# Message passing layer on one core: transposes at the end of TensorE's last nine steps, own banks for the last node layers and sums

## The chip, the cores and the metric

The kernel runs on one core of a Trainium2 chip. The time is what the device takes for one execution, in microseconds, and the result for a kernel is the median of its runs. All numbers are float32.

## The reference

A graph has 12,500 nodes with 64 features and 200,000 edges, sorted by destination. Cut to what matters:

```python
def ssp(x): return softplus(x) - log(2)
nodes = x[edges].reshape(200000, 128)            # source row, destination row
gates = ssp(edge_attr @ We1 + be1) @ We2 + be2
gates = gates * (1 - sigmoid(5 * (edge_weight1 - 3.5)))
h = ssp(nodes @ Wn1 + bn1) @ Wn2 + bn2
message_sum = zeros((12500, 64)).at[dst].add(h * gates)
new = x + (ssp(message_sum @ Ws1 + bs1) @ Ws2 + bs2)
out = layernorm(x + new, axis=-1, eps=1e-5)
```

## The kernel before

**Steps.** The edges are worked off in 391 quads of 512 (NQ = 391; the last has 320 edges). The five engines run their own programs, written out by hand in the order in which each executes, and meet at semaphores. In step s the engines work on neighbouring quads:

- GpSimd gathers the source rows of a quad from DRAM with four indirect DMAs (L449) into a ring of 16 places (`ga`), up to 15 quads ahead of the transposes.
- SyncE loads edge features (`ea`), the destinations relative to a window (`relb`) and the windows' shares of the first node layer (`bw`), two quads at a time.
- TensorE: `transposes(q)` (L561 for edge features, L563 for gathered rows) into bank 4 of PSUM, `front(q)` (L609, the first node layer of the edge, and the gates' first layer in `gates_in`, L571), `mid(q)` (second layers, L622 and L626) into bank 6 or 5, and `back(q)` (L639), which sums the messages of a quad over a window of 64 nodes by a one-hot matrix, into bank 7.
- ScalarE: `evacuate(q)` copies the transposed quad to SBUF (L818), `sizes(q)` (L826, L828) and `logs(q)` (L835 to L841) work out the softplus of the first layers, `fill(q)` (L847) writes the biases of the second layers into their bank.
- VectorE: `pick` (L1062) and `one_hot` (L1068) make the one-hot matrices, `hidden(q)` (L1076, L1080) the first layers' output, `message(q)` (L1087, L1095) the product with the gates, and `flush(q)` (L1114) adds the window's sums to `acc`, at a place that is read from a table (L1102).

TensorE's step s is front(s), transposes(s + 2), back(s - 3), mid(s - 1). ScalarE's step s is sizes(s), evacuate(s + 2), logs(s), fill(s).

**Node layer.** The nodes are in 25 groups of 500 (NG = 25). Since edges are sorted, a group is complete long before the last edge, and from step 206 (NODE0) each eight steps (STEPS) carry the node layer of one group: in the step at offset 0 TensorE's `node_hidden` (L648), between the front's L609 and its gates L571, with ScalarE's `node_sizes` (L886, L887) and `node_log` (L891, L893) in the same step; at offset 2 VectorE's `node_hidden` (L1194); at offset 3 TensorE's `node_out` (L657), at 4 VectorE's `node_add` (L1200), at 5 ScalarE's square (L897), at 6 VectorE's sum (L1204) and ScalarE's root (L902, L904), at 7 VectorE's scaling (L1212 to L1220). SyncE then stores the group.

**The tail.** Steps up to 381 run in loops; steps 382 (TAIL0) to 393 are written out. Step 382 is offset 0 of group 22, step 390 offset 0 of group 23, whose other pieces, and group 24 (the last), follow after the last step. Group 24's node layer needs the sums of all quads. The sums are in `ps_s` (bank 7), node_hidden writes into banks 0 and 1 behind the columns of the even quads' first layers (`ps_h`), node_out into banks 2 and 3 behind those of the odd quads (`ps_y`). The end of TensorE's program:

```python
                for s in range(TAIL0, NQ + 3):
                    fast_step(s, s % ARING, group_at(s))
                node_out(NG - 2)
                pe.wait_ge(flushed, NQ)
                node_hidden(NG - 1)
                node_out(NG - 1)
```

A branch for inputs that are not sorted closely enough (`general_step`) isn't taken here.

## Time and profile before

| | before |
|---|---|
| median of 3 runs | 2000.88 us (2000.53 to 2002.76) |
| the profiled execution | 2002.99 us, its span 2001.1 us |
| TensorE busy, mean granted clock | 1730.7 us (86%), 0.953 |
| ScalarE busy | 1532.0 us (77%) |
| GpSimd busy | 1485.6 us (74%) |
| VectorE busy | 1285.7 us (64%) |
| last gather begins | 1966.65 us |

The profile lists for each engine when its instructions began, in us from the start of the span, and what ended the idle time before them. In such a row a group of like instructions stands as one ("x8"). A duration in a row can overlap the start of the next operation on the same engine by up to 0.13 us; where the text speaks of the time that an operation takes of its engine's queue, it is the distance to the next start. "issue" as a releaser means that the profile shows nothing that was waited for. The granted clock of TensorE is 1.0 at 2.4 GHz and 0.5 at 1.2 GHz.

### The profile page before, as it was taken

To read this page: it belongs to the slowest core of one execution; us is meant where nothing else is said; L and a number is where in the kernel's file an instruction comes from. 1 tells how busy PE (TensorE), PEld (TensorE's weight loads), DVE (VectorE), ACT (ScalarE), POOL (GpSimd) and SP (SyncE) were. 2 spreads that over 40 slices of the span, in tenths; PEclk is the share of its full clock that TensorE was granted. 3 is DMA by queue.
4 is the path that set the end of the run, shared out by engine and by line. 5 is a ranking of instruction groups with operands and counts; after the bars stand their busy time and mean duration, and the time that the engine had idled before them with its cause. 6 is when DMAs were issued, how large, how long until landed. Compare 5 with 4: busy or idle time off the path is not lost.

```text
span 2001.1 us, 53540 instructions
## 1 busy us (share of the span) xinstructions
PE 1730.7 (86%) x16249; PEld 1323.6 (66%) x16249; DVE 1285.7 (64%) x3512; ACT 1532.0 (77%) x3368; POOL 1485.6 (74%) x1572
## 2 busy tenths in 40 slices
PE   4699999888888888888889889888888988898887
PEld 3477777766666666666666666666666666666665
DVE  4578887666665655566656666666666666666665
ACT  2589998877777777777777877787878777787785
POOL 6777777777777777777777777777777777777772
PEclk7799999999899999999999999999999999999998
DMA  5433343333333333333333333333333333333331
GB/s 120 121 86 97 96 96 97 84 85 83 80 76 70 74 73 72 73 72 73 72 73 74 77 76 71 78 76 70 81 75 74 73 76 73 71 82 75 73 74 31
DMA packets 255904, 157.77 MB, mean 79 GB/s; under 512 B 44873, under 2 KB 226518, under 8 KB 255838
## 3 DMA queue, kind: packets, MB, share of 16 engines
q1 hardware_dynamic: 202124, 104.94, 18.0%
q0 software_dynamic: 50048, 51.35, 15.9%
q10 hardware_dynamic: 3666, 0.68, 0.2%
q8 instruction: 32, 0.52, 0.1%
q14 instruction: 34, 0.28, 0.0%
HBM read 146.94 MB, written 9.87 MB: 78 GB/s over the span
## 4 chain that ended last, share of the span: by engine, by line
POOL 59%; issue 22%; PE 11%; DVE 3%; SPq 2%; ACT 1%; DMA 1%; ACTq 1%; DVEq 1%; POOLq 0%
POOL ga L449 59%; PE ps L609 3%; PE ps L622 3%; PE ps L626 1%; SPq L331 1%; PE ps L571 1%; PE ps L561 1%; PE ps L639 1%; DVE hid L1076 1%; DMA ga<-in_x_dram,srcT 1%; DVE hid L1080 1%; PE ps L563 1%; DMA w_tab<-w_i 0%; SPq L326 0%; SPq L317 0%
## 5 line engine op out<-in xcount | busy, mean ns | idle before, releaser
L449 POOL DMA_INDIRECT ga<-in_x_dram,srcT x1564 | 1484.6, 949 | 481.3 <-issue 473.0
L826 ACT ACTIVATE lg<-ps,bn1c 128x512 f32<-128x512 f32 x391 | 268.5, 687 | 305.3 <-PE ps L571 272.8
L622 PE MATMUL ps<-wn,hid 128*128 128x64 f32 x3128 | 445.1, 287 | 19.2 <-DVE hid L1080 16.5
L1076 DVE SCALAR_TENSOR_TENSOR hid<-ps,neg_b,lg 128x512 f32<-128x512 f32 x391 | 292.9, 749 | 228.5 <-ACT lg L841 214.4
L622 PEld LDWEIGHTS ps<-wn,hid 128*128 128x128 f32 x3128 | 390.2, 196 | 51.2 <-DVE hid L1080 24.9
L561 PE MATMUL ps<-ident,ea 128*128 128x128 f32 x782 | 172.4, 303 | 216.8 <-DMA ga<-in_x_dram,srcT 147.8
L818 ACT COPY xe<-ps 128x512 f32<-128x512 f32 x391 | 229.9, 588 | 124.0 <-PE ps L563 109.0
L609 PE MATMUL ps<-xe,wn 64*128 64x256 f32 x1564 | 289.5, 449 | 0.0
L561 PEld LDWEIGHTS ps<-ident,ea 128*128 128x128 f32 x782 | 79.8, 143 | 301.5 <-issue 283.9
L626 PE MATMUL ps<-we,hid 128*128 128x128 f32 x1564 | 272.2, 299 | 0.0
L1114 DVE TENSOR_TENSOR acc<-acc,ps 64x64 f32 x782 | 168.2, 215 | 161.8 <-issue 155.3
L1068 DVE TENSOR_TENSOR oh<-ps,relT 128x256 f32<-128x256 f32 x391 | 163.9, 419 | 164.7 <-PE ps L639 144.0
L835 ACT ACTIVATE lg<-lg 128x512 f32<-128x512 f32 x391 | 251.8, 644 | 0.0
L609 PE MATMUL ps<-ohT,bw 64*128 64x256 f32 x1564 | 246.9, 394 | 0.0
L839 ACT ACTIVATE lg<-lg 128x512 f32<-128x512 f32 x391 | 245.7, 628 | 0.0
L847 ACT COPY ps<-bsum 128x512 f32<-128x512 f32 x391 | 232.6, 595 | 0.0
L626 PEld LDWEIGHTS ps<-we,hid 128*128 128x128 f32 x1564 | 216.9, 201 | 0.0
L1080 DVE SCALAR_TENSOR_TENSOR hid<-ps,neg_b,lg 128x256 f32<-128x256 f32 x391 | 185.7, 475 | 0.0
L1062 DVE TENSOR_SCALAR ohT<-relb,iota_p 128x256 f32<-128x256 uint8 x391 | 148.6, 380 | 55.5 <-PE ps L571 48.9
L828 ACT ACTIVATE lg<-ps,be1c 128x256 f32<-128x256 f32 x391 | 182.8, 467 | 0.0
L639 PE MATMUL ps<-oh,msg 128*64 128x64 f32 x3128 | 179.6, 237 | 1.3 <-DVE acc L1114 1.3
L571 PE MATMUL ps<-xe,we 64*64 64x128 f32 x3128 | 180.6, 302 | 0.0
(124 smaller groups left out, 1848.5 us busy)
## 6 DMA issues: line engine op xcount, KB each, us to landing
ea<-in_edge_attr_dram SPq DMA_DIRECT2D x195, 256.0 KB
ga<-in_x_dram,srcT POOLq DMA_INDIRECT x1564
bw<-b_tab SPq DMA_DIRECT2D x782, 32.0 KB
relb<-rel_tab SPq DMA_DIRECT2D x196, 64.0 KB
b_tab<-share SPq DMA_DIRECT2D x25, 250.0 KB
out_dram<-xs SPq DMA_DIRECT2D x25, 125.0 KB
xs<-in_x_dram SPq DMA_DIRECT2D x3, 750.0 KB
rows_i<-in_dst_dram SPq DMA_DIRECT2D x1, 768.0 KB
```

The source lines that it names most:

```text
L449: pool.indirect_dma_start(to[:, t % 2, t // 2, :], None, x, bass.IndirectOffsetOnAxis(ap=idx[:, t:t + 1], axis=0)).then_inc(done, 16)
L561: pe.transpose(ps_xe[:, k * P:(k + 1) * P], ea[:, u, k, :], ident[:, :])
L609: pe.matmul(ps[:, 2 * (u % 2) + k, 0:PAIR], weights, rows, start=(end == 0), stop=(end == 1), skip_group_check=True)
L622: pe.matmul(hg[:, t * D:(t + 1) * D], hid[:, u % 2, t * P:(t + 1) * P], wn2[:, :], start=False, stop=False, skip_group_check=True)
L626: mm = pe.matmul(gates[:, :, j, :], hid[:, u % 2, QUAD + j * P:QUAD + (j + 1) * P], we2[:, :].rearrange("p (k d) -> p k d", k=2), start=Fa ...
L818: act.copy(xe[:, u, :, :].rearrange("p h e -> p (h e)"), ps_xe[:, :]).then_inc(xe_e, 1)
L826: act.activation(lg[:, u % 2, 0:QUAD].rearrange("p (k e) -> p k e", k=2), z[:, :, 0:PAIR], ACT.Abs, bias=bn1c[:, 0:1]).then_inc(n_abs, 1)
L835: act.activation(ln_n, ln_n, ACT.Exp, scale=-1.0).then_inc(n_exp, 1)
L839: act.activation(ln_n, ln_n, ACT.Ln, bias=1.0)
L847: act.copy(hg, bsum[:, :, :, :].rearrange("p h k d -> p (h k d)")).then_inc(filled, 1)
L1076: dve.scalar_tensor_tensor(out=hid[:, u % 2, 0:QUAD].rearrange("p (k e) -> p k e", k=2), in0=ps[:, 2 * (u % 2):2 * (u % 2) + 2, 0:PAIR], s ...
L1080: dve.scalar_tensor_tensor(out=hid[:, u % 2, QUAD:QUAD + PAIR].rearrange("p (j e) -> p j e", j=2), in0=ps[:, 2 * (u % 2):2 * (u % 2) + 2, ...
```

## The change

In TensorE's steps 382 to 390 the transposes move to the end of the step and are those of the next quad instead of the one after it; step 382 has none, since step 381 already made those of 383. ScalarE's copy moves in the same way behind fill and node step. Step 390 carries no node step any more. The node layer of group 23 comes after back(388) on TensorE and writes into banks 2 and 3 (`ps_h_end`), its outputs into 0 and 1 (`ps_y_end`); the sums of quad 390 go to bank 4 (`ps_s_end`), which the transposes no longer need. VectorE loads the places of the last three quads together and takes the last operations in a new order.

```diff
+        ps_h_end = ps[:, 2:4, 3 * P:3 * P + PB]
+        ps_y_end = ps[0:PB, 0:2, 3 * P:4 * P]
+        ps_s_end = ps[:, 4, :]
...
-            def back(q, u):
+            def back(q, u, sums=ps_s):
...
-                if reached(q, 1):
+                if reached(q, 1) and sums is ps_s:
                     pe.wait_ge(flushed, q)
...
-                for s in range(TAIL0, NQ + 3):
-                    fast_step(s, s % ARING, group_at(s))
-                node_out(NG - 2)
+                for s in range(TAIL0, NQ):
+                    front(s, s % ARING, group_at(s) if s < NQ - 1 else None)
+                    back(s - 3, (s - 3) % RING)
+                    mid(s - 1, (s - 1) % RING, ps_hg[(s - 1) % 2])
+                    if TAIL0 < s < NQ - 1:
+                        transposes(s + 1, (s + 1) % ARING)
+                back(NQ - 3, (NQ - 3) % RING)
+                pe.wait_ge(flushed, NQ - 1 - BACK)
+                node_hidden(NG - 2, ps_h_end)
+                back(NQ - 2, (NQ - 2) % RING)
+                mid(NQ - 1, (NQ - 1) % RING, ps_hg[(NQ - 1) % 2])
+                node_out(NG - 2, ps_y_end)
+                back(NQ - 1, (NQ - 1) % RING, ps_s_end)
                 pe.wait_ge(flushed, NQ)
-                node_hidden(NG - 1)
-                node_out(NG - 1)
+                pe.wait_ge(h_relu, NG - 1)
+                node_hidden(NG - 1, ps_h_end)
+                node_out(NG - 1, ps_y_end)
...
                 for q in range(TAIL0, NQ):
-                    fast_step(q, q % RING, group_at(q))
+                    node = group_at(q) if q < NQ - 1 else None
+                    sizes(q, q % RING)
+                    if node is not None and node[1] == 0:
+                        node_sizes(node[0])
+                    logs(q, q % RING)
+                    fill(q, ps_hg[q % 2], 2)
+                    if node is not None:
+                        node_step(*node)
+                    if TAIL0 < q < NQ - 1:
+                        evacuate(q + 1, (q + 1) % RING)
+                node_sizes(NG - 2, ps_h_end)
+                node_log(NG - 2)
                 node_square(NG - 2)
-                node_sizes(NG - 1)
+                node_sizes(NG - 1, ps_h_end)
...
-                for s in range(TAIL0, NQ + 3):
+                for s in range(TAIL0, NQ):
                     fast_step(s, s % RING, group_at(s))
-                node_add(NG - 2)
+                load_places(NQ - 3, 3)
+                message(NQ - 2, (NQ - 2) % RING, ps_hg[(NQ - 2) % 2])
+                one_hot(NQ - 1, (NQ - 1) % RING)
+                flush(NQ - 3, 0)
+                hidden(NQ - 1, (NQ - 1) % RING)
+                flush(NQ - 2, 1)
+                node_hidden(NG - 2)
+                message(NQ - 1, (NQ - 1) % RING, ps_hg[(NQ - 1) % 2])
+                flush(NQ - 1, 2, ps_s_end)
+                node_add(NG - 2, ps_y_end)
                 node_sum(NG - 2)
                 node_hidden(NG - 1)
                 node_scale(NG - 2)
-                node_add(NG - 1)
+                node_add(NG - 1, ps_y_end)
```

TensorE in step 388 before: front (L609, L571), transposes of quad 390 (L561, L563), back(385) (L639), mid(387) (L622, L626). `ps` is PSUM; the other names are the operands.

```order
L609 MATMUL ps<-xe,wn 128x256 x2
L609 MATMUL ps<-ohT,bw 128x256 x2
L571 MATMUL ps<-xe,we 64x128 x4
L561 MATMUL ps<-ident,ea 128x128 x2
L563 MATMUL ps<-ident,ga 128x128 x2
L639 MATMUL ps<-oh,msg 64x64 x4
L622 MATMUL ps<-wn,hid 128x64 x4
L626 MATMUL ps<-we,hid 128x2x64 x2
```

The same step after: front (L613, L575), back(385) (L643), mid(387) (L626, L630), then the transposes of quad 389 (L565, L567), and the next front.

```order
L613 MATMUL ps<-xe,wn 128x256 x2
L613 MATMUL ps<-ohT,bw 128x256 x2
L575 MATMUL ps<-xe,we 64x128 x4
L643 MATMUL ps<-oh,msg 64x64 x4
L626 MATMUL ps<-wn,hid 128x64 x4
L630 MATMUL ps<-we,hid 128x2x64 x2
L565 MATMUL ps<-ident,ea 128x128 x2
L567 MATMUL ps<-ident,ga 128x128 x2
L613 MATMUL ps<-xe,wn 128x256 x2
L613 MATMUL ps<-ohT,bw 128x256 x2
```

The transposes have moved from before back and mid to behind them, and are of one quad less ahead.

ScalarE in step 388 before: sizes (L826, L828), the copy of quad 390 (L818), logs (L835 to L841), fill (L847), the root of group 22 (L902, L904).

```order
L826 ACTIVATE lg<-ps,bn1c 128x512
L828 ACTIVATE lg<-ps,be1c 128x256
L818 COPY xe<-ps 128x512
L835 ACTIVATE lg<-lg 128x512
L837 ACTIVATE lg<-lg 128x256
L839 ACTIVATE lg<-lg 128x512
L841 ACTIVATE lg<-lg 128x256
L847 COPY ps<-bsum 128x512
L902 ACTIVATE lvar<-svar,epsb 125x4
L904 ACTIVATE rstd<-lvar 125x4
```

The same step after: sizes (L842, L844), logs (L851 to L857), fill (L863), root (L918, L920), then the copy of quad 389 (L834), and the next step's first operation.

```order
L842 ACTIVATE lg<-ps,bn1c 128x512
L844 ACTIVATE lg<-ps,be1c 128x256
L851 ACTIVATE lg<-lg 128x512
L853 ACTIVATE lg<-lg 128x256
L855 ACTIVATE lg<-lg 128x512
L857 ACTIVATE lg<-lg 128x256
L863 COPY ps<-bsum 128x512
L918 ACTIVATE lvar<-svar,epsb 125x4
L920 ACTIVATE rstd<-lvar 125x4
L834 COPY xe<-ps 128x512
L842 ACTIVATE lg<-ps,bn1c 128x512
```

The copy has moved from between sizes and logs to behind everything of the step, and is of the quad whose front comes next.

TensorE's last part before, from the node layer inside front 390 on (L648 is node_hidden, L657 node_out; "L639 x8" are back(389) and back(390)):

```order
L648 MATMUL ps<-acc,ws1d 128x125 x4
L571 MATMUL ps<-xe,we 64x128 x4
L639 MATMUL ps<-oh,msg 64x64 x4
L622 MATMUL ps<-wn,hid 128x64 x4
L626 MATMUL ps<-we,hid 128x2x64 x2
L639 MATMUL ps<-oh,msg 64x64 x4
L622 MATMUL ps<-wn,hid 128x64 x4
L626 MATMUL ps<-we,hid 128x2x64 x2
L639 MATMUL ps<-oh,msg 64x64 x8
L657 MATMUL ps<-ws2d,hidn 125x128 x2
L648 MATMUL ps<-acc,ws1d 128x125 x4
L657 MATMUL ps<-ws2d,hidn 125x128 x2
```

After, from the end of front 390, back(387), on (L652 is node_hidden, L661 node_out):

```order
L643 MATMUL ps<-oh,msg 64x64 x4
L626 MATMUL ps<-wn,hid 128x64 x4
L630 MATMUL ps<-we,hid 128x2x64 x2
L643 MATMUL ps<-oh,msg 64x64 x4
L652 MATMUL ps<-acc,ws1d 128x125 x4
L643 MATMUL ps<-oh,msg 64x64 x4
L626 MATMUL ps<-wn,hid 128x64 x4
L630 MATMUL ps<-we,hid 128x2x64 x2
L661 MATMUL ps<-ws2d,hidn 125x128 x2
L643 MATMUL ps<-oh,msg 64x64 x4
L652 MATMUL ps<-acc,ws1d 128x125 x4
L661 MATMUL ps<-ws2d,hidn 125x128 x2
```

node_hidden of group 23 has gone from inside the front of step 390 to behind back(388), mid(390) has come behind back(389), and back(390) behind node_out.

## Rows read from the trace of the kernel before

**Rows 1.** The page: chain that ended last by engine; costliest group of instructions.

```profile
POOL 59%; issue 22%; PE 11%; DVE 3%; SPq 2%; ACT 1%; DMA 1%; ACTq 1%; DVEq 1%; POOLq 0%
...
L449 POOL DMA_INDIRECT ga<-in_x_dram,srcT x1564 | 1484.6, 949 | 481.3 <-issue 473.0
```

**Rows 2.** Timeline (start us, us, instruction, idle before), GpSimd's last gather; transposes on TensorE.

```profile
1966.65 0.94 POOL L449 DMA_INDIRECT ga<-in_x_dram,srcT  x1 [0.30 <-issue]
...
1960.69 0.41 PE L561 MATMUL ps<-ident,ea 128*128 128x128 f32 x2 [1.02 <-issue]
...
1969.16 0.41 PE L561 MATMUL ps<-ident,ea 128*128 128x128 f32 x2 [0.53 <-issue]
```

**Rows 3.** Timeline, TensorE: transposes(383); front 389, back, mid, front 390.

```profile
1935.19 0.44 PE L561 MATMUL ps<-ident,ea 128*128 128x128 f32 x2
...
1971.63 0.70 PE L609 MATMUL ps<-xe,wn 64*128 64x256 f32 x4
...
1973.08 0.45 PE L639 MATMUL ps<-oh,msg 128*64 128x64 f32 x8
1973.46 1.11 PE L622 MATMUL ps<-wn,hid 128*128 128x64 f32 x8
...
1974.99 0.70 PE L609 MATMUL ps<-xe,wn 64*128 64x256 f32 x4
```

**Rows 4.** Windows: stretch, engines' busy us (x instructions), PEclk, DMA share, GB/s.

```profile
1980.00:1990.00 10.00, 6.28 (x46) 5.52 (x45) 4.89 (x16) 3.18 (x8) 0.00 (x0) 0.64 0.00 0
```

**Rows 5.** Timeline, TensorE's last part.

```profile
1983.18 1.97 PE L622 MATMUL ps<-wn,hid 128*128 128x64 f32 x8 [2.41 <-DVE hid L1080]
...
1986.04 0.70 PE L639 MATMUL ps<-oh,msg 128*64 128x64 f32 x8
...
1989.68 1.97 PE L648 MATMUL ps<-acc,ws1d 128*128 128x125 f32 x8
1993.83 1.22 PE L657 MATMUL ps<-ws2d,hidn 128*125 128x128 f32 x4 [2.19 <-DVE hidn L1194]
```

**Rows 6.** Timeline, VectorE: hidden(390), message(390), last operation.

```profile
1982.65 0.48 DVE L1080 SCALAR_TENSOR_TENSOR hid<-ps,neg_b,lg 128x256 f32<-128x256 f32 x1
...
1986.61 0.42 DVE L1095 TENSOR_TENSOR msg<-ps,gcut 128x256 f32<-128x256 f32 x1
...
1997.60 0.42 DVE L1220 TENSOR_TENSOR xs<-xs,rsq 125x256 f32<-125x256 f32 x1
```

**Rows 7.** Timeline, ScalarE in steps 387 to 389.

```profile
1968.33 0.42 ACT L897 ACTIVATE sq<-xs 125x256 f32<-125x256 f32 x1
...
1969.82 0.58 ACT L818 COPY xe<-ps 128x512 f32<-128x512 f32 x1
...
1971.97 0.59 ACT L847 COPY ps<-bsum 128x512 f32<-128x512 f32 x1
1972.48 0.29 ACT L902 ACTIVATE lvar<-svar,epsb 125x4 f32<-125x4 f32 x1
1972.81 0.20 ACT L904 ACTIVATE rstd<-lvar 125x4 f32<-125x4 f32 x1
1973.21 0.69 ACT L826 ACTIVATE lg<-ps,bn1c 128x512 f32<-128x512 f32 x1 [0.20 <-PE ps L571]
...
1975.81 0.59 ACT L847 COPY ps<-bsum 128x512 f32<-128x512 f32 x1
```

**Rows 8.** Timeline, ScalarE: first operation of step 383.

```profile
1946.31 0.67 ACT L826 ACTIVATE lg<-ps,bn1c 128x512 f32<-128x512 f32 x1
```

**Rows 9.** Timeline, TensorE: node output of group 22 in step 385.

```profile
1953.31 0.70 PE L657 MATMUL ps<-ws2d,hidn 128*125 128x128 f32 x4
```

**Rows 10.** Timeline, TensorE: first and last of 80 gaps of 1.2 us; a window.

```profile
336.54 0.44 PE L561 MATMUL ps<-ident,ea 128*128 128x128 f32 x2 [1.29 <-DMA ga<-in_x_dram,srcT]
...
1929.69 0.43 PE L561 MATMUL ps<-ident,ea 128*128 128x128 f32 x2 [1.24 <-DMA ga<-in_x_dram,srcT]
...
1932.00:1934.00 2.00, 2.00 (x10) 1.60 (x11) 1.35 (x3) 1.53 (x5) 1.58 (x2) 0.50 0.21 33
```

More of the change, by code:

```diff
@@ L638, in back, with node_hidden @@
                     for k in range(2):
-                        mm = pe.matmul(ps_s[k * D:(k + 1) * D, 0:W], msg[:, u % 2, 2 * k + j, :],
+                        mm = pe.matmul(sums[k * D:(k + 1) * D, 0:W], msg[:, u % 2, 2 * k + j, :],
                                        oh[:, u, 2 * k + j, :], start=(j == 0), stop=(j == 1))
                 mm.then_inc(sc_mm, 1)
-            def node_hidden(g):
+            def node_hidden(g, hidden_units=ps_h):
                 sums = acc[:, bass.ds(g * GN, GN)].rearrange("f (p b) -> f b p", b=4)
@@ L647, in node_hidden, with node_out @@
                     for c in range(2):
-                        mm = pe.matmul(ps_h[:, c, :], ws1d[:, h, :, :].rearrange("f i d -> f (i d)"), sums[:, 2 * h + c, :],
+                        mm = pe.matmul(hidden_units[:, c, :], ws1d[:, h, :, :].rearrange("f i d -> f (i d)"), sums[:, 2 * h + c, :],
                                        start=(h == 0), stop=(h == 1), skip_group_check=True)
                 mm.then_inc(h_mm, 1)
-            def node_out(g):
+            def node_out(g, y=ps_y):
                 pe.wait_ge(h_b, g + 1)
@@ L656, in node_out @@
                 for c in range(2):
-                    mm = pe.matmul(ps_y[:, c, :], hidn[:, c * PB:(c + 1) * PB],
+                    mm = pe.matmul(y[:, c, :], hidn[:, c * PB:(c + 1) * PB],
                                    ws2d[:, :, :].rearrange("f h d -> f (h d)"), start=True, stop=True)
@@ L1104, in load_places, with flush @@
                     skip_runtime_bounds_check_because=IN_RANGE)
-            def flush(q, at):
+            def flush(q, at, sums=ps_s):
                 firsts = places[2 * at:2 * at + 2]
@@ L1114, in flush @@
                     ins = dve.tensor_tensor(acc[half, bass.ds(firsts[k], W)], acc[half, bass.ds(firsts[k], W)],
-                                            ps_s[half, 0:W], ALU.add)
+                                            sums[half, 0:W], ALU.add)
                 ins.then_inc(flushed, 1)
@@ L1199, in node_add @@
                 rows = xs[0:PB, bass.ds(g * 4, 4), :].rearrange("p (h c) d -> p c h d", c=2)
-                dve.tensor_tensor(rows, ps_y.rearrange("p c (h d) -> p c h d", h=2), rows, ALU.add).then_inc(y_add, 1)
+                dve.tensor_tensor(rows, y.rearrange("p c (h d) -> p c h d", h=2), rows, ALU.add).then_inc(y_add, 1)
             def node_sum(g):
```

8 lines of the change are left out of this document (4 added, 4 removed).

## The prediction

> **What bounds the kernel now.** I read the page first, then the windows, then the timelines of the last 70 us engine by engine. The page's chain gives GpSimd 59%: the pace is one gather after another, 0.95 us busy and 0.30 us of issue, four to a step, 5.0 us a step [rows 1, 2]. The last gather starts at 1966.65 and its quad (390) is transposed at 1969.16, 2.51 us later; for quad 388, whose last gather started two steps of 5.0 earlier, that distance was 4.03 us (to 1960.69) [rows 2]. What follows the last gather, 34.5 us to the end of the span, has no gather to wait for. There the reader is to see three pieces: fronts 389 and 390, which follow each other on TensorE without a gap (1971.63, 1974.99) [rows 3]; the end of the pipe, where TensorE idles 2.41 us before mid(390), the mean granted clock is 0.64, and matmuls run at 1.2 GHz (L622 takes 1.97 us instead of 1.11) [rows 3 to 5]; and the node layer of the last group, from L648 at 1989.68 to VectorE's last operation at 1997.60 + 0.42 = 1998.02 [rows 5, 6]. 3.08 us of store follow to 2001.1.
>
> **The change, part 1: transposes last, evacuation last.** Before, TensorE transposes quad s + 2 inside step s, and ScalarE copies it (L818) between sizes and logs of step s: ready a whole step before its front, so no front waits for it. After, the transposes of s + 1 stand at the end of step s, and ScalarE copies them after logs and fill of s. So front(s + 1) waits for a copy that stands behind all of ScalarE's work of step s, and that work waits for front(s). This closes a loop, priced by rows. From the start of a front to ScalarE's first operation on it: 1971.63 to 1973.21, 1.58 us [rows 3, 7]. Sizes and logs, 1973.21 to 1975.81, 2.60; the fill L847, 1971.97 to 1972.48, 0.51; the copy L818 0.58, and 0.04 until TensorE sees it (as from the end of L1080 at 1983.13 to L622 at 1983.18), 0.62 [rows 5 to 7]. The loop is 1.58 + 2.60 + 0.51 + 0.62 = **5.31 us** a step. TensorE's own work in a step is front 1.45, back 0.38, mid 1.53, transposes about 0.6: they end 3.96 us after the front's start, ahead of the copy's turn at 4.69 [rows 2, 3]. So ScalarE's order decides, and TensorE idles about 1.35 us in each step.
>
> Where it starts: TensorE's step 382 has the same front and node layer in both kernels. ScalarE no longer has a copy in step 382 (0.58, of which 0.11 overlap the next operation), so sizes(383) begin at 1946.31 - 0.47 = 1945.84 [rows 7, 8]. Sizes, logs, fill, + 3.11, and the copy, + 0.62: front(384) at 1949.57. Then six loops of 5.31 to front(390), and on the same path the node output of group 22 in step 385 (L657, 0.70 less 0.07 of overlap), the square L897 (0.42 less 0.06) and the root, L902 and L904 (1972.48 to 1972.81 + 0.20, and a hand-over of 0.04) [rows 7, 9]: 1949.57 + 31.86 + 0.63 + 0.36 + 0.57 = **1982.99**, against 1974.99: 8.0 us later. By then quad 390 has been in SBUF for over 10 us: that a late gather no longer holds back TensorE's other work is worth nothing here, since a loop of 5.31 is no faster than the gathers' 5.0.
>
> **Part 2: the node layer of group 23 out of step 390.** Before, L648 stood between front and gates of 390, 1.97 us as at 1989.68 [rows 5]; after, it comes behind back(388). ScalarE's start on quad 390 goes from 1974.99 + 1.97 + 1.58 = 1978.54 to 1982.99 + 1.58 = 1984.57: of the 8.0 us, 6.0 are left.
>
> **Part 3: the order of the last sums.** By TensorE's new order, from front(390)'s end at 1984.43: back(387) 0.38, mid(389) 1.53, back(388) 0.38, L648 1.97, back(389) 0.38, to 1989.07. mid(390) needs hid(390): ScalarE's logs end at 1984.57 + 2.60 + 0.14 of tail = 1987.31, but VectorE first does message(389), one-hot(390) and flush(388) behind mid(389)'s end at 1986.34, some 1.7 us, and then 1.15 for L1076 and L1080: 1989.25. TensorE waits 0.2 instead of 2.41 us, stays at 2.4 GHz, and mid(390) takes 1.53 instead of the 2.86 from L622 at 1983.18 to L639 at 1986.04 [rows 5]: to 1990.78. The node output waits for VectorE's hidn until about 1990.8 and ends at 1991.45. message(390), two operations of 0.42 and their hand-over, ends near 1991.76 [rows 6], back(390) at 1992.25, flush(390) 0.5 later, and L648 of the last group starts at **1992.8** against 1989.68. So this part gives back 2.9 of the 6.0 us: 1.3 by the clock in mid(390), the rest because sums and node layer lie in what was idle. The bank of its own for the last sums takes away back(390)'s wait for flush(389), which ends before message(390) does: nothing. What hides it is message(390); without that cover it were 0.5.
>
> From L648 to VectorE's end, 8.34 us before [rows 5, 6], nothing is reordered; the doubt is L657, 1.22 at 1.2 GHz, 0.70 at 2.4 [rows 5, 9]. The end is + 2.6 to + 3.1; I take + 2.9.
>
> **Part 4: the clock.** Before, TensorE's gaps stood in the loop of the gathers, which hid a slow spell. In the trace TensorE idled at least 1.2 us in one piece 80 times between 336 and 1930 us, first and last in [rows 10]; after 23 of them the granted clock fell from 1.0 to 0.5 within 4 us, as after the last (0.50 in the window from 1932), and stayed there 4 to 6 us. The new loop has seven gaps of 1.1 to 1.9 us: by that share two falls, and fewer because a slow step fills its own gap. A fall now lies on the path. At 1.2 GHz mid takes 2.86, back 0.70 and transposes and gates about twice their time, 1.0 and 0.6 [rows 5]; with the fall one us into a front, the transposes end at 1.06 + 0.6 + 0.70 + 2.86 + 1.0 = 6.2 us after its start instead of the copy's turn at 4.69: + 1.5, and up to 2.4 if the next front is slow too. I take one fall, + 1.5.
>
> The Trainium skill ("TensorE: Matmul & The Clock Gate", section "HAM oscillation — how this bites in real kernels") has it that only idle stretches longer than any in this loop bring the clock down. By that rule no fall would come and the time would be 2003.3, rival 1 below; the last gap of [rows 10], 1.24 us and the clock down behind it, speaks against it.
>
> **Part 5: the start.** In this execution TensorE came out of a slow spell into step 382. transposes(383) ran at 1935.19; its last gather began seven steps of 5.0 before 1966.65, at 1931.65, and by the distances 2.51 and 4.03 it could have run at 1934.2 to 1935.7 [rows 2, 3]. The new loop passes such a shift on, the old one absorbed it: between - 1.0 and + 0.5, I take - 0.5.
>
> **Sum.** 2.9 + 1.5 - 0.5 = + 3.9 us. The profiled execution took 2002.99 us for a span of 2001.1, and the median of the runs is 2.1 lower, 2000.88; the difference of the tails is added to the median: **2004.8**.
>
> **Rivals.**
> 1. No fall of the clock in the new loop: 2000.88 + 2.4 = 2003.3. For it: 57 of the 80 gaps passed without.
> 2. Two or more falls: 2004.8 + 1.5 = 2006.3, three 2007.8. For it: a gap in every step, longest where square and root are added. It decides from the second fall on.
> 3. The faster side: the loop is hidden, because ScalarE is through with a step before the transposes of the next are. If the fronts stay where they are, front(390) at 1974.99, parts 2 and 3 are pure gain, 8.0 - 2.9 = 5.1 us: 1995.8. If they come as soon as the transposes allow (1969.16 + 0.6 + 0.62 = 1970.4), it is 4.6 us less, 1991.2. The draw lies at front(390) = 1980.1, a loop of (1980.1 - 1949.57 - 1.56) / 6 = 4.83 us; faster by over 4 us needs 4.2. For it: fronts 389 and 390 were 3.36 us apart in the old order [rows 3]. Against: no copy stood between them, and ScalarE's rows alone hold 3.7 of the loop, the front 1.58 [rows 7].
> 4. The loop is some tenths shorter than my sum, near those 4.83: 2000.9, no change. It needs an overlap that no row shows.
>
> **How the numbers follow.** Forecast, one fall: 0.33; rival 1: 0.25; rival 2: 0.31; rival 3: 0.05; rival 4: 0.06. A measurement of this kernel tells 0.2%, 4.0 us, from no change. The forecast lies at that bound; I put 0.18 of its 0.33 within and 0.15 beyond. Within: 0.18 + 0.25 + 0.06 = 0.49; slower: 0.15 + 0.31 = 0.46; faster 0.05. Range: down to rival 1 with the start's - 1.0 and the end's + 2.6, which is 2002.5, and one us less for the spread of a median, 2001.5; up to three falls of which one is of the dearer kind, 2009.
>
> **What would show it.** In the changed kernel the copies L834 begin behind the fill L863 in steps 383 to 389, TensorE idles 1.1 to 1.9 us before each front, the fronts are 5.3 us apart and front(390) starts about 16 us behind the last gather; TensorE waits under 0.7 us for hid(390). Fronts under 4.6 us apart, or idle time there that ends at a gather, would prove the forecast wrong; a clock of 1.0 throughout with 5.3 a step is rival 1.

## The result

The changed kernel takes **2011.2 us** (median of 8 runs, 2005.8 to 2016.5), the kernel before 2000.7 us (8 runs, 2000.0 to 2002.8). The ratio of their runs is 1.0046 with a 95% interval of 1.0037 to 1.0055: slower, and clear of noise (the two medians by themselves give 1.0052). The forecast was 2004.8 us with a range up to 2009. The direction of its sum was right, the size was not: + 3.9 us forecast, + 10.5 measured by the medians.

The profiled execution of the changed kernel took 2007.65 us (span 2004.8), one of the shorter ones. Its rows show the loop of the forecast almost to the hundredth. TensorE's fronts in the timeline (start us, us, instruction, the idle time before it and what ended it):

```profile
1946.88 0.70 PE L613 MATMUL ps<-xe,wn 64*128 64x256 f32 x4 [1.63 <-ACT xe L834]
...
1952.21 0.70 PE L613 MATMUL ps<-xe,wn 64*128 64x256 f32 x4 [1.47 <-ACT xe L834]
...
1958.18 0.70 PE L613 MATMUL ps<-xe,wn 64*128 64x256 f32 x4 [1.47 <-ACT xe L834]
...
1963.51 0.70 PE L613 MATMUL ps<-xe,wn 64*128 64x256 f32 x4 [1.47 <-ACT xe L834]
...
1969.14 0.76 PE L613 MATMUL ps<-xe,wn 64*128 64x256 f32 x4 [1.76 <-ACT xe L834]
```

From 1958.18 to 1963.51 is 5.33 us, and each front now waits for ScalarE's copy. On ScalarE the same step:

```profile
1959.76 0.69 ACT L842 ACTIVATE lg<-ps,bn1c 128x512 f32<-128x512 f32 x1 [1.63 <-PE ps L575]
...
1962.35 0.59 ACT L863 COPY ps<-bsum 128x512 f32<-128x512 f32 x1
1962.87 0.59 ACT L834 COPY xe<-ps 128x512 f32<-128x512 f32 x1
```

The copy follows the fill and ScalarE then waits 1.6 us for the next front: neither engine is full, each waits for the other. Before, the same fronts had no gap in front of them [rows 3]. Behind the fifth of these gaps the clock fell; the windows (columns as in [rows 4]) and the rows of two slow steps:

```profile
1960.00:1970.00 10.00, 6.77 (x66) 5.63 (x64) 6.18 (x17) 7.46 (x17) 4.78 (x5) 0.98 0.14 30
1970.00:1980.00 10.00, 9.32 (x62) 6.56 (x61) 4.40 (x15) 5.01 (x12) 0.00 (x0) 0.51 0.04 13
```

```profile
1971.94 1.97 PE L626 MATMUL ps<-wn,hid 128*128 128x64 f32 x8
...
1976.40 1.23 PE L613 MATMUL ps<-xe,wn 64*128 64x256 f32 x4 [0.68 <-ACT xe L834]
...
1982.93 0.70 PE L613 MATMUL ps<-xe,wn 64*128 64x256 f32 x4 [1.13 <-ACT xe L834]
```

These two steps took 7.26 us (from 1969.14) and 6.53 us, where 5.75 and 5.33 are due: 2.7 us lost by one fall (5.75 and 5.33 us are the lengths of the same two steps in e7, e14 and e17 below, where the clock stayed at 2.4 GHz). The end of the kernel, which answers to [rows 5]:

```profile
1989.48 1.10 PE L626 MATMUL ps<-wn,hid 128*128 128x64 f32 x8 [0.39 <-DVE hid L1107]
...
1992.15 0.45 PE L643 MATMUL ps<-oh,msg 128*64 128x64 f32 x8 [0.56 <-DVE msg L1122]
1993.24 2.04 PE L652 MATMUL ps<-acc,ws1d 128*128 128x125 f32 x8 [0.64 <-DVE acc L1141]
1997.47 1.22 PE L661 MATMUL ps<-ws2d,hidn 128*125 128x128 f32 x4 [2.19 <-DVE hidn L1221]
```

mid(390) waits 0.39 us instead of 2.41 and runs in 1.10 instead of 1.97; L652 starts 10.3 us after front 390 (1982.93), against 14.7 before. The last gather, on GpSimd:

```profile
1965.05 0.94 POOL L453 DMA_INDIRECT ga<-in_x_dram,srcT  x1 [0.30 <-issue]
```

The span of 2004.8 us ended 39.75 us behind it, against 34.45 before: 5.3 us longer.

### The profile page after: what moved, and what is told of

Read it like the earlier page. It is cut to its first block, busy times and chain, and to the rows that moved or that the text cites. A ratio compares the mean times of both kernels' runs of the same rounds, so it can differ in the third digit from the quotient of the medians.

```text
span 2004.8 us, 53539 instructions
## 1 busy us (share of the span) xinstructions
PE 1744.5 (87%) x16249; PEld 1333.0 (66%) x16249; DVE 1286.6 (64%) x3512; ACT 1532.5 (76%) x3368; POOL 1484.1 (74%) x1572
## 3 DMA queue, kind: packets, MB, share of 16 engines
q0 software_dynamic: 50048, 51.35, 14.8%
## 4 chain that ended last, share of the span: by engine, by line
POOL 57%; issue 21%; PE 11%; DVE 3%; ACT 3%; DMA 2%; SPq 1%; ACTq 1%; DVEq 1%; POOLq 0%
POOL ga L453 57%; PE ps L613 3%; PE ps L626 2%; DMA ga<-in_x_dram,srcT 1%; PE ps L630 1%; PE ps L575 1%; SPq L335 1%; DVE hid L1103 1%; PE ps L565 1%; DVE hid L1107 1%; PE ps L643 1%; PE ps L567 1%; ACT xe L834 0%; ACT lg L851 0%; PE ps L652 0%
## 5 line engine op out<-in xcount | busy, mean ns | idle before, releaser
L842 ACT ACTIVATE lg<-ps,bn1c 128x512 f32<-128x512 f32 x391 | 268.7, 687 | 321.1 <-PE ps L575 286.7
L626 PE MATMUL ps<-wn,hid 128*128 128x64 f32 x3128 | 449.1, 288 | 21.0 <-DVE hid L1107 19.3
L626 PEld LDWEIGHTS ps<-wn,hid 128*128 128x128 f32 x3128 | 394.1, 198 | 53.8 <-DVE hid L1107 30.2
L565 PE MATMUL ps<-ident,ea 128*128 128x128 f32 x782 | 173.2, 304 | 196.8 <-DMA ga<-in_x_dram,srcT 143.0
L834 ACT COPY xe<-ps 128x512 f32<-128x512 f32 x391 | 230.1, 589 | 114.8 <-PE ps L567 101.3
L613 PE MATMUL ps<-xe,wn 64*128 64x256 f32 x1564 | 292.3, 452 | 9.6 <-ACT xe L834 9.6
L630 PE MATMUL ps<-we,hid 128*128 128x128 f32 x1564 | 274.4, 300 | 0.0
L565 PEld LDWEIGHTS ps<-ident,ea 128*128 128x128 f32 x782 | 80.5, 143 | 280.0 <-issue 263.6
L851 ACT ACTIVATE lg<-lg 128x512 f32<-128x512 f32 x391 | 251.9, 644 | 0.0
L613 PE MATMUL ps<-ohT,bw 64*128 64x256 f32 x1564 | 249.0, 397 | 0.0
L863 ACT COPY ps<-bsum 128x512 f32<-128x512 f32 x391 | 232.9, 596 | 0.0
L630 PEld LDWEIGHTS ps<-we,hid 128*128 128x128 f32 x1564 | 219.0, 202 | 0.0
L844 ACT ACTIVATE lg<-ps,be1c 128x256 f32<-128x256 f32 x391 | 182.9, 468 | 0.0
L643 PE MATMUL ps<-oh,msg 128*64 128x64 f32 x3128 | 180.8, 238 | 0.6 <-DVE msg L1122 0.6
L575 PE MATMUL ps<-xe,we 64*64 64x128 f32 x3128 | 181.1, 303 | 0.0
```

What stands on the lines that cost most here:

```text
L565: pe.transpose(ps_xe[:, k * P:(k + 1) * P], ea[:, u, k, :], ident[:, :])
L613: pe.matmul(ps[:, 2 * (u % 2) + k, 0:PAIR], weights, rows, start=(end == 0), stop=(end == 1), skip_group_check=True)
L626: pe.matmul(hg[:, t * D:(t + 1) * D], hid[:, u % 2, t * P:(t + 1) * P], wn2[:, :], start=False, stop=False, skip_group_check=True)
L630: mm = pe.matmul(gates[:, :, j, :], hid[:, u % 2, QUAD + j * P:QUAD + (j + 1) * P], we2[:, :].rearrange("p (k d) -> p k d", k=2), start=Fa ...
L834: act.copy(xe[:, u, :, :].rearrange("p h e -> p (h e)"), ps_xe[:, :]).then_inc(xe_e, 1)
L842: act.activation(lg[:, u % 2, 0:QUAD].rearrange("p (k e) -> p k e", k=2), z[:, :, 0:PAIR], ACT.Abs, bias=bn1c[:, 0:1]).then_inc(n_abs, 1)
```

## The experiments

The chips differ. On the first and on chip 14 the kernel before takes 2001 to 2003 us, on chips 6, 11 and 15 it takes 2512 to 2544 us, with no gather in the way at the end. So each kernel is compared with runs of the kernel before on its own chip. What can be compared across chips are the steps of the tail: at the same clock, and with no gather in the way, they have the same length to 0.02 us everywhere. The table gives, from the profile of each, the time from front 382 to front 390, from there to the last group's node layer on TensorE (L648 before, L652 after), from there to the end of the span, and their sum; then the time of the runs against the kernel before on that chip.

| run | kernel | 382 to 390 | to L652 | to end | sum | ratio (95%) |
|---|---|---|---|---|---|---|
| before | before, first chip | 37.3 | 14.7 | 11.4 | 63.4 | |
| e5 | before, chip 15 | 34.6 | 13.8 | 11.0 | 59.4 | 0.9989 (0.9973 to 1.0004) |
| after | changed, 1 fall | 47.9 | 10.3 | 11.6 | 69.8 | 1.0046 (1.0037 to 1.0055) |
| e1 | changed, 2 falls, chip 11 | 49.2 | 10.3 | 11.5 | 71.0 | 1.0043 (1.0028 to 1.0059) |
| e6 | changed, 1 short fall, chip 15 | 46.4 | 10.3 | 11.6 | 68.3 | 1.0049 (1.0027 to 1.0071) |
| e13 | changed, 1 short fall, chip 11 | 46.3 | 10.3 | 11.5 | 68.2 | 1.0057 (1.0036 to 1.0078) |
| e16 | changed, slow for 5 of 8 steps, chip 6 | 53.6 | 14.8 | 11.6 | 79.9 | 1.0034 (1.0020 to 1.0049) |
| e2 | + 4 fillers, chip 11 | 46.0 | 10.3 | 11.5 | 67.8 | 1.0035 (1.0020 to 1.0050) |
| e7 | + 3 fillers, chip 15 | 45.2 | 10.3 | 11.5 | 67.1 | 1.0022 (1.0005 to 1.0039) |
| e14 | + 3 fillers, chip 11 | 45.2 | 10.3 | 11.5 | 67.0 | 1.0023 (1.0013 to 1.0034) |
| e17 | + 3 fillers, chip 6 | 45.2 | 10.3 | 11.5 | 67.0 | 1.0021 (1.0007 to 1.0036) |
| e11 | new steps, old end, chip 14 | 53.5 | 14.5 | 11.5 | 79.5 | 1.0052 (1.0038 to 1.0066) |
| e3 | old steps, new end, chip 11 | 34.6 | 10.8 | 11.5 | 56.9 | 0.9990 (0.9977 to 1.0004) |
| e12 | the same, 1 fall, chip 14 | 39.0 | 10.8 | 11.5 | 61.3 | 0.9984 (0.9975 to 0.9993) |
| e4 | one ahead, early copy, chip 11 | 34.4 | 10.8 | 11.5 | 56.7 | 0.9986 (0.9968 to 1.0003) |
| e8 | the same, chip 15 | 34.4 | 10.8 | 11.5 | 56.8 | 0.9986 (0.9971 to 1.0002) |
| e15 | the same, chip 11 | 34.4 | 10.8 | 11.5 | 56.7 | 0.9997 (0.9987 to 1.0007) |
| e18 | late transposes, early copy, chip 6 | 44.5 | 11.5 | 11.5 | 67.5 | 1.0024 (1.0008 to 1.0040) |

**The changed kernel again (e1, e6, e13, e16).** No edit.

> The changed kernel once more, for another profile of it: eight executions took 2005.8 to 2016.5 us, and the profiled one (2007.65) had one stretch of TensorE at 1.2 GHz in the tail, 1969.7 to 1979.7 us. Theory A (the clock is on the path since the gaps stand in the loop): the excess over 2000.7 us follows the time that TensorE spends at 1.2 GHz after 1940 us; at 2.4 GHz the loop is 5.33 us a step in every execution; an execution near 2011 shows some 20 us of half clock there, one near 2016 nearly all of the tail. Theory B (something else differs between executions, the landing of gathers or the state in which step 382 begins): the slow executions show longer waits on DMA or a later front 382, with the clock as in the profile that we have. Median expected 2008 to 2012 by both.

> The changed kernel on the same chip. In its two profiles the tail from front 382 to the end of the span was 69.8 and 71.0 us, with one stretch at 1.2 GHz each (and a short second one in the later), and each such stretch cost 2.2 us (two steps of 6.94 and 6.53 us instead of 5.90 and 5.33). Theory A (clock falls add up): ratio 1.004 to 1.005, and this profile's tail is 67.6 us + 2.2 us for each fall that it shows; the spread of the executions is 2.2 us steps wide. Theory B (something outside the tail): the tail is 67.6 to 70 us long in an execution that lasts 2010 us or more.

> The changed kernel beside the next two on one chip. By e9 and e10 a step of the new loop costs 1.02 us more on average through the clock (7.00 us against 5.98), so seven steps cost 7.1 us over the 2.6 us that the loop and the new end cost at 2.4 GHz: 2010.4 us and ratio 1.0049 on a chip like the first.

> The changed kernel beside the next two on one chip, as e13. Ratio 1.0046 to 1.0057; by the clock's 1.02 us a step 2010.4 us on a chip like the first.

The chips were not like the first, so the medians of 2010 us were not met; the ratios were, apart from e16's 1.0034, which is lower than expected. Where e6's expectation counts 2.2 us for a fall (a tail of 69.8 us with one), its profile has 68.3 us with one fall, which cost 1.2 us. Theory B of e1, longer waits on DMA, shows in none of these profiles: each gap before a front from 384 on ends at ScalarE's copy.

The profiles of e6 and e13 are of the shortest of their executions. e1's is of one near the median, and the tail accounts for it: 71.0 us is 11.6 more than the 59.4 of the kernel before (e5), and the medians differ by 11.5. In e6 and e13 the tails are 8.9 and 8.8 us longer, while these executions lie only 3.5 and 3.8 us above the median of the kernel before on their chips; its own executions spread over 10 to 25 us there. e16's profile is of a long execution, 2534.2 us where the chip's median for the kernel before is 2512.4. Its rows show where such an execution loses:

```profile
2491.59 0.70 PE L613 MATMUL ps<-xe,wn 64*128 64x256 f32 x4 [1.76 <-ACT xe L834]
...
2493.66 1.97 PE L626 MATMUL ps<-wn,hid 128*128 128x64 f32 x8
...
2498.12 1.22 PE L613 MATMUL ps<-xe,wn 64*128 64x256 f32 x4 [0.68 <-ACT xe L834]
...
2505.84 1.22 PE L613 MATMUL ps<-xe,wn 64*128 64x256 f32 x4 [0.68 <-ACT xe L834]
...
2509.10 1.97 PE L626 MATMUL ps<-wn,hid 128*128 128x64 f32 x8
```

After the gap of 1.76 us the clock falls inside the step; the next step is 7.72 us long (2498.12 to 2505.84), and TensorE is not full in it either: 0.68 us before each of its two fronts are left. The windows say 0.79, 0.50, 0.86, 0.65, 0.50 and 0.50 from 2460 on in tens of us; two of them:

```profile
2480.00:2490.00 10.00, 8.65 (x80) 6.35 (x76) 4.27 (x12) 6.16 (x14) 0.00 (x0) 0.86 0.04 10
...
2500.00:2510.00 10.00, 9.32 (x62) 7.08 (x61) 3.22 (x9) 5.15 (x11) 0.00 (x0) 0.50 0.04 12
```

The tail of this execution is 12.9 us longer than one without a fall (79.9 against 67.0), 8.4 of it in the steps and 4.5 behind front 390, where the clock was still down. It is 20.5 us longer than e5's, and the execution 21.8 us above the chip's median for the kernel before. Falls of the clock are enough to explain a long execution; that they explain each of them isn't shown, since only profiled ones have rows.

**Fillers (e2, e7, e14, e17).** Extra matmuls in the gap, three or four a step (here four):

```diff
                     if TAIL0 < s < NQ - 1:
                         transposes(s + 1, (s + 1) % ARING)
+                        for k in range(4):
+                            pe.matmul(ps[:, 2 * ((s + 1) % 2) + k % 2, 0:PAIR], ident[:, :],
+                                      bsum[:, :, :, :].rearrange("p h k d -> p (h k d)")[:, 0:PAIR],
+                                      start=True, stop=True, skip_group_check=True)
```

> The changed kernel with four more matmuls of 128 x 256 (about 1.06 us at 2.4 GHz, as the four of a front take) at the end of each of TensorE's steps 383 to 389, behind the transposes, in the gap in which it waits for ScalarE's copy (1.47 us); they write into first-layer columns that the next front overwrites. Theory A: TensorE's gaps shrink to 0.4 us, the clock stays at 2.4 GHz to the end of the steps, the loop stays 5.33 us, and the time is 2003.0 us (range 2002 to 2004.5) with a spread under 2 us. Theory B: the fillers change nothing, median near 2010 and spread as in the changed kernel; should they cost time, it is at most 7 x 0.4 us more.

> As e2_filler but with three extra matmuls a step. Four took 1.83 us a step instead of the 1.06 that I had reckoned, more than the gap of 1.47, and made the loop 5.53 us instead of 5.33; the clock was 1.00 through all steps. Three take 1.4 us and fit into the gap. Theory A: clock 1.00 to the end of the steps, loop 5.33, tail from front 382 to the end 66.8 us, and 2003.0 us on a chip like the first (ratio 1.0012), with a spread no wider than that of the kernel before. Theory B: ratio as that of the changed kernel, 1.0045.

> The changed kernel with three extra matmuls in each of TensorE's steps 383 to 389. If the clock is the rest of the loss in the nine steps themselves, and not only in the long loop of e9 and e10, it is 7 us faster than e13 on the same chip although it does more work: 2003.3 to 2004 us and ratio 1.0013 to 1.0017 on a chip like the first, with a spread of 2 us instead of 10. If the rest of the loss in these nine steps is something else (the start of step 382, what lies around the span), it is as slow as e13.

> The fillers once more, hoped to be on a chip of the first kind, where executions of the kernel before lie within 4 us: 2003.3 to 2004 us there, 7 us under e16, spread 2 to 3 us. On a chip of the other kind 1.0022 again (1.0022 and 1.0023 so far). If the rest of the loss in the nine steps is not the clock, as slow as e16.

In all four profiles the clock stayed at 1.00 through the steps, and with three fillers the tail was 67.1, 67.0 and 67.0 us. e7's rows, L746 being the fillers:

```profile
2491.36 1.46 PE L746 MATMUL ps<-bsum,ident 128*128 128x256 f32 x6
2493.41 0.70 PE L613 MATMUL ps<-xe,wn 64*128 64x256 f32 x4 [0.59 <-ACT xe L838]
```

```profile
2460.00:2480.00 20.00, 18.35 (x171) 14.56 (x172) 12.65 (x34) 14.44 (x33) 0.00 (x0) 1.00 0.13 38
2480.00:2500.00 20.00, 18.60 (x166) 14.36 (x163) 12.08 (x33) 13.76 (x32) 0.00 (x0) 1.00 0.04 12
```

Each filled kernel had the lower median beside its unfilled one: 2550.9 against 2555.1 us, 2520.7 against 2527.1, 2551.5 against 2555.6, 2519.3 against 2524.2, so 4.2, 6.4, 4.1 and 4.9 us less for 21 or 28 matmuls more (4 fillers took longer than the gap and made a step 5.53 us instead of 5.33). By the ratios the differences are 0.0008 to 0.0034, and the intervals of each pair overlap; the four agree in sign. Filled, the kernel is still 6.0 to 7.3 us slower than the kernel before on these chips, by the medians: the loop at 2.4 GHz alone makes the tail 67.0 us instead of 59.4. The 7 us that I expected of the fillers were not reached, and a chip of the first kind, on which it could have been seen in one pair, did not come up.

**The new loop in 185 steps (e9, e10).** The same order from step 206 on, without and with three fillers a step:

```diff
-                if not known or s + 2 < NQ:
+                late = node is not None
+                if not late and (not known or s != NODE0 - 1):
                     transposes(s + 2, (v + 2) % ARING)
                 if not known or s >= 3:
                     back(s - 3, (u - 3) % RING)
                 if not known or 1 <= s <= NQ:
                     mid(s - 1, (u - 1) % RING, ps_hg[(u - 1) % 2])
+                if late:
+                    transposes(s + 1, (v + 1) % ARING)
...
-                if not isinstance(q, int) or q + 2 < NQ:
+                if node is None and (not isinstance(q, int) or q != NODE0 - 1):
                     evacuate(q + 2, (u + 2) % RING)
                 logs(q, u)
                 fill(q, ps_hg[u % 2], 2)
...
                 if node is not None:
                     node_step(*node)
+                    evacuate(q + 1, (u + 1) % RING)
```

> The changed kernel with the new order (transposes of s + 1 at the step's end, ScalarE's copy behind the fill) not only in steps 382 to 390 but from step 206 on, 185 steps instead of 9, so that one profile shows how often the clock falls in this loop and what a fall costs. Theory A: steps of 5.33 us, with node layer 8 x 5.33 + 5.0 = 47.7 us for a group of eight (40.0 by the gathers on the first chip, some 37 where no gather holds it), and falls as often as in the three profiled tails (3 to 4 in 21 steps, 2.3 us each): 25 to 35 falls and 60 to 80 us of loss in 185 steps. On a chip like the first 2165 us + 60 to 80 us = 2225 to 2245 us. Theory B (the excess is outside this loop): few falls, under 20 us from them.

> The same with three extra matmuls behind the transposes in each of these steps (1.4 us in a gap of 1.47, as in e7_filler3). Theory A: the clock stays at 1.0 from step 206 on, a group takes 47.7 us, and the kernel is 60 to 80 us faster than e9_loop_everywhere on the same chip, although it does more work. Theory B: not faster than it.

This is the experiment that decides. Both ran on chip 14, of the first kind: 2369.9 us without fillers (three runs, 2345.3 to 2371.6), **2183.3 us with them** (2181.3 to 2183.7), ratios 1.179 and 1.090. 552 matmuls more, three in each of 184 steps, make the kernel 187 us faster, 1.0 us a step. Windows of 1000 and 900 us in the loop, and 700 us of the kernel before; the last number but two is the granted clock:

e9:

```profile
1200.00:2200.00 1000.00, 792.90 (x5949) 608.54 (x5948) 476.03 (x1290) 572.58 (x1274) 560.43 (x594) 0.76 0.22 55
```

e10:

```profile
1200.00:2100.00 900.00, 826.31 (x7149) 648.38 (x7149) 498.11 (x1350) 597.41 (x1337) 577.50 (x612) 1.00 0.26 63
```

before:

```profile
1200.00:1900.00 700.00, 618.31 (x5782) 470.93 (x5782) 450.66 (x1260) 553.11 (x1235) 530.14 (x558) 0.98 0.33 75
```

The clock is 0.76 in the new loop, so about half of its time is spent at 1.2 GHz, and 1.00 as soon as the gap is filled. By the fronts' starts, a step took 7.00 us on average (156 steps) without and 5.98 us (151 steps) with fillers. The expected 60 to 80 us were far too few: 187.

The rows of e9 also tell why. From 1200 to 2290 us TensorE at 2.4 GHz idled at least 1.2 us in one piece 94 times, and the clock fell after 34 of them. That is 0.36 a gap, not far from the 23 of 80 in the kernel before. But a slow stretch lasted 15 us on average and up to 48, where in the kernel before none lasted 8. In this one each step has its gap of some 0.7 us and the clock stays down, 0.50 in the window from 1234 to 1258:

```profile
1238.98 1.23 PE L613 MATMUL ps<-xe,wn 64*128 64x256 f32 x4 [0.76 <-ACT xe L837]
...
1246.71 1.22 PE L613 MATMUL ps<-xe,wn 64*128 64x256 f32 x4 [0.67 <-ACT xe L837]
```

At 1.0 us a step, over the 155 steps of that window, a fall cost 4.6 us.

**Part 1 alone (e11).**

```diff
-                for s in range(TAIL0, NQ + 3):
-                    fast_step(s, s % ARING, group_at(s))
+                for s in range(TAIL0, NQ):
+                    front(s, s % ARING, group_at(s))
+                    back(s - 3, (s - 3) % RING)
+                    mid(s - 1, (s - 1) % RING, ps_hg[(s - 1) % 2])
+                    if TAIL0 < s < NQ - 1:
+                        transposes(s + 1, (s + 1) % ARING)
+                for s in range(NQ, NQ + 3):
+                    fast_step(s, s % ARING, group_at(s))
                 node_out(NG - 2)
```

with ScalarE's steps as in the change, the node step of 390 kept.

> Part 1 of the change alone: transposes and copies late in steps 382 to 390, but the node layer still in step 390 and the end as before. Front 382 to front 390 takes 45.2 us and 2.3 more for each fall, from front 390 to the last group's node layer 13.8 us as before (15 with a fall there), and the tail from front 382 to the end 70.2 us + falls, against 67.1 + falls in the changed kernel and 59.4 (no gather in the way) or 63.4 before. Ratio 1.0045 to 1.0065, above the changed kernel's. If the new end rather than the steps were what costs, it would be 1.000 to 1.002.

On chip 14: 2013.8 us against 2002.6, ratio 1.0052. So the steps alone cost 11 us. Its profile is of the longest of its five executions (2019.8 us) and shows 53.5 us from front 382 to 390, 8.3 over the loop at 2.4 GHz, with 0.57 in the window

```profile
1950.00:1970.00 20.00, 18.31 (x117) 14.08 (x118) 9.35 (x26) 9.44 (x21) 14.26 (x15) 0.57 0.27 61
```

**Part 2 and 3 alone (e3, e12).** The new end with the old steps:

```diff
                 for s in range(TAIL0, NQ):
                     front(s, s % ARING, group_at(s) if s < NQ - 1 else None)
+                    if s + 2 < NQ:
+                        transposes(s + 2, (s + 2) % ARING)
                     back(s - 3, (s - 3) % RING)
                     mid(s - 1, (s - 1) % RING, ps_hg[(s - 1) % 2])
-                    if TAIL0 < s < NQ - 1:
-                        transposes(s + 1, (s + 1) % ARING)
```

and ScalarE's copy of q + 2 between sizes and logs.

> Only the new end: steps 382 to 390 of TensorE and ScalarE as before the change (transposes of s + 2 behind the front, the copy between sizes and logs), but no node layer in step 390, and everything behind the last step in the changed kernel's order with its banks. Theory A (the moved transposes and copies are the whole loss, the new end a gain of about 5 us): fronts stay where they were, front 390 8.3 us after the last gather's start, the last group's node layer (L648 before) 4.9 us earlier, and 1995.5 us (1994.5 to 1997). A rival, that the new end is worth nothing on its own because mid(390) waits for ScalarE anyway: 2000 to 2001.

> The new end alone once more. Its profile on the second chip had a tail of 56.9 us, 2.5 us under the 59.35 of the kernel before on the third: 3.0 us less from front 390 to the last node layer (10.8 against 13.8), 0.5 more behind it. Expected ratio 0.9989 (0.998 to 1.000) where no gather holds the tail, and 0.9975 on a chip like the first, where the kernel before lost the clock in mid(390) (14.7 us instead of 13.8).

On chip 14: **1999.6 us** against 2002.6, ratio 0.9984 (0.9975 to 0.9993): faster than the kernel before, and than the new steps alone (e11) on the same chip; the changed kernel itself did not run there. On chip 11 (e3, ratio 0.9990) the interval includes 1, and the changed kernel took 14 us more (e1). The gain on chip 14 is 3.1 us, not 5. Its last gather begins at 1966.13 and the span ends 31.3 us behind it, 34.5 before. Of the 4.9 us expected at the last node layer 3.9 came (10.8 us after front 390 instead of 14.7, I had 9.8), and on the way front 390 came 9.0 us after the last gather's start instead of 8.3. This execution had a fall of the clock too, behind a gap of 1.64 us in step 384: two steps took 6.80 and 6.52 us, where e3's took 4.34 and 4.58. In the old order TensorE caught up with the gathers again before front 390.

**One quad ahead with the early copy (e4, e8, e15).**

```diff
                 for s in range(TAIL0, NQ):
                     front(s, s % ARING, group_at(s) if s < NQ - 1 else None)
+                    if TAIL0 < s < NQ - 1:
+                        transposes(s + 1, (s + 1) % ARING)
                     back(s - 3, (s - 3) % RING)
                     mid(s - 1, (s - 1) % RING, ps_hg[(s - 1) % 2])
-                    if TAIL0 < s < NQ - 1:
-                        transposes(s + 1, (s + 1) % ARING)
```

with ScalarE's copy of q + 1 between sizes and logs.

> The new end, and in steps 382 to 390 the transposes only one quad ahead as in the changed kernel, but right behind the front instead of at the step's end, and ScalarE's copy between sizes and logs instead of behind the fill. If the place of the copy behind the logs is the cause, and not that the transposes are only one quad ahead, the loop is TensorE's own 3.95 us or ScalarE's 4.3, a step waits for its gather again at the end, front 390 starts about 6 us after the last gather's start (8.3 before) and the time is 1993.5 us (1992 to 1996). If being one quad ahead is the cause, the loop stays above 5 us and the time above 2000.

> Once more the new end with transposes one quad ahead right behind the front and the copy between sizes and logs. On the second chip its tail was 56.7 us from front 382 and the ratio 0.9986 with an interval too wide to tell. On a chip like the first the last gathers hold it: front 390 some 6 us behind the last gather's start, 1993.5 us (1992 to 1996), ratio 0.9964. On one like the second 0.9985 again.

> The new end with transposes one quad ahead right behind the front and the early copy, for the first time on a chip like the first if it is one: the last gathers then hold its last steps only through the transposes of 390. e12 (the new end with the old steps) gave 0.9984 there. If releasing TensorE from waiting one quad earlier for its gathers is worth what the change meant it to be, it is 1 to 3 us better, ratio 0.997 to 0.998; if the steps are no faster for it, 0.9984 again.

All three ran where no gather holds the tail. Steps of 3.95 us, as long as in the kernel before on such a chip (e5), and no gap before a front: that the transposes are one quad ahead instead of two costs nothing. Whether it gains anything where gathers bound the kernel was not measured; 0.9986, 0.9986 and 0.9997 do not tell it from e3's 0.9990.

**Late transposes with the early copy (e18).** The changed kernel, with ScalarE's copy of q + 1 put back between sizes and logs.

> The changed kernel with ScalarE's copy of s + 1 between sizes and logs again, while TensorE's transposes stay at the end of the step. If the copy's place behind logs and fill were all that costs, the loop would shrink from 5.33 to near 4.7. By the rows it can't: the copy now makes the logs wait for the transposes, the logs the first layers' output, this mid, and mid the next transposes: 0.47 + 1.66 + 0.14 + 1.15 + 0.04 + 1.53 + 0.60 + 0.11 = 5.7 us a step, front 382 to front 390 about 47 to 48 us without a fall. Then late transposes are as costly as the late copy, ratio 1.004 to 1.006.

Ratio 1.0024, below the 1.004 to 1.006 expected, and steps of 5.55 us, not 5.7: hardly shorter a way from front 382 to 390 than in the changed kernel (44.5 against 45.2 us). The loop now closes the other way round:

```profile
2487.10 1.10 PE L626 MATMUL ps<-wn,hid 128*128 128x64 f32 x8 [0.94 <-DVE hid L1107]
...
2489.18 0.59 ACT L834 COPY xe<-ps 128x512 f32<-128x512 f32 x1 [1.84 <-PE ps L567]
...
2489.82 0.70 PE L613 MATMUL ps<-xe,wn 64*128 64x256 f32 x4 [0.68 <-ACT xe L834]
```

ScalarE waits 1.84 us for the transposes, and TensorE 0.94 us for VectorE and 0.68 us for the copy. So it isn't the copy's place alone: the late transposes are enough to close a loop. Its two shorter gaps made no fall in the profiled execution; one profile does not show that they never do.

**The kernel before (e5).**

> The kernel before, for a profile on the same chip as the next three. On the chip of the last four runs the kernel before took 2543.6 us and no gather held it in the tail, on the first chip 2000.7. Expected: 2000.7 us with front 390 about 8.3 us after the last gather's start if this chip is like the first, or some 2543 us with fronts 382 to 390 about 32 us apart in all (3.95 to 4.6 a step, 1.96 more in step 382) and the end some 60.5 us after front 382 if it is like the second. Ratio 1.000 in both.

The ratio, 0.9989 (0.9973 to 1.0004), agrees with 1. The profile shows steps of 3.95 us where no gather stands in the way:

```profile
2465.87 0.70 PE L609 MATMUL ps<-xe,wn 64*128 64x256 f32 x4
...
2469.82 0.70 PE L609 MATMUL ps<-xe,wn 64*128 64x256 f32 x4
...
2473.77 0.70 PE L609 MATMUL ps<-xe,wn 64*128 64x256 f32 x4
```

I had expected a tail of 60.5 us; it is 59.4.

## Why the prediction was wrong in size

**The bound and the loop: right.** The copy behind the fill, a front that waits for it, 5.31 us a step forecast and 5.33 measured in every profile of the new order; front 382 to 390 at 2.4 GHz 45.3 us forecast and 45.2 measured (e7, e14, e17). e11 against e12 gives the cause by its parts: the new steps alone 1.0052, the new end alone 0.9984 on the same chip.

**The node layer out of step 390 and the new end: right in kind, 0.5 us off.** L652 comes 10.3 us after front 390, I had 9.8. mid(390) started 0.3 us later than by my sum (VectorE began the hid of 390 at 1988.28, 2.0 us behind mid(389)'s end, where I had 1.7). From the end of message(390) to L652 it took 1.24 us (1992.00 to 1993.24), where I had 1.04.

**The last 8.3 us: the worse end of the doubt.** L661 took 1.22 us, at 1.2 GHz, in each profile, after a gap of 2.19. Only e5, the kernel before, had 0.70 there (L657).

**The start: right in kind.** The last gather began 30.0 us after front 382 in the changed kernel's profile, 28.95 before: TensorE came 1.1 us earlier to its tail, just past the end of my - 1.0 to + 0.5.

Up to here the sum is + 2.5 us at 2.4 GHz: tail 67.0 less 30.0, 37.0, against 34.45. My rival 1 had + 2.4. The forecast fails in one term.

**The clock: the failed step.** Part 4 took one fall at 1.5 us. With the 2.5 us above, 8.0 of the measured 10.5 us are left for this term. Its three factors:

1. *How often: roughly right a gap, cut by half for a wrong reason.* The share of the kernel before, 23 falls after 80 gaps, gives two falls for seven gaps, and e9's 34 of 94 gives 2.5. I then took one, "because a slow step fills its own gap". It does not: in e16 and e9 a slow step is 7.72 us long and still leaves a gap of 0.68 us. The five profiles of the changed kernel show one, two, one, one and two falls (e16 last); it is not their number that makes e16 long.
2. *How long: the size that was most wrong.* I priced a slow stretch of 4 to 6 us, as in the kernel before (mean clock 0.96 from 336 to 1930 us). In the loop with a gap in each step it lasted 15 us on average, and the clock was 0.76 (e9). A duration that was read in one pattern of gaps did not carry over to a denser one.
3. *How much each.* A fall cost 2.7 us in the first profile, where two steps were slow. It cost 1.2 and 2.8 us in e1, 1.2 in e6 and 1.1 in e13, all near my 1.5 and 2.4. In e9 it cost 4.6 us, and in e16 the two slow stretches cost 12.9 us together.

With the 1.0 us a step of e9 and e10, the seven steps behind gaps give + 7.1 us, and 2000.7 + 2.5 + 7.1 = 2010.3, against 2011.2 measured. That is an estimate: it carries a rate of 184 steps over to seven. In the nine steps themselves the fillers took 4.1 to 6.4 us away, on other chips, which would give 2007.3 to 2009.6. By both, the clock is a larger term on the first chip than the loop's 2.5 us. On chips 6, 11 and 15, where no gather held the kernel before in its tail, the loop itself costs 7.6 us and the clock is the smaller part. Whether all of the rest on the first chip is the clock stays open, as no execution over 2007.65 us was profiled there.

The chances put 0.31 on two or more falls (2006.3, three 2007.8), and the range ended at 2009 with three; it should have asked what happens if a slow stretch holds on. The Trainium skill ("TensorE: Matmul & The Clock Gate", section "HAM oscillation — how this bites in real kernels") has as its rule to leave no idle pieces on TensorE that are longer than any in this loop. The trace shows that this is not enough to keep the clock up: 0.51 in the window from 1970 us, behind a gap of 1.76 us. Rival 1, built on no fall at all, fell: each of the five profiles of the changed kernel has one.

**Rivals 3 and 4** fell: no front came under 5.3 us after another.

## What to carry to other kernels

Do not order a producer behind all the work of the step before the one that it feeds. Two engines that each have slack (here 3.95 and 3.7 us of work) then wait for one another, and the step is the front's 1.6 us plus all of ScalarE's 3.7 instead of the longer of the two. Moving ScalarE's copy back is not enough when TensorE's transposes stay last (e18). If such a loop leaves a gap on TensorE in each step, price the whole loop at 1.2 GHz as well, and take that as the bound of the range; a cheap test is to fill the gap with matmuls, since a kernel that gets faster by more work, at a higher granted clock, has shown its cause. Parts of a change that pull in opposite directions should be tried apart: here the new end alone took 1999.6 us against 2002.6, while the whole change made the kernel slower.
